# Attention and int8 feed-forward block: Q and K projected transposed, V in one pass, softmax sums through DRAM, loops unrolled

## The chip, the core and the metric

The kernel runs on one core of one Trainium2 chip, written in Bass: each engine has its own instruction stream, ordered only by semaphores. PE is TensorE, DVE is VectorE, ACT is ScalarE, POOL is GpSimd, SP is SyncE, which issues most DMAs. The metric is device time in microseconds (us), lower is better.

## The reference

X has shape (4, 1024, 512): batch, rows, columns. With 16 query heads, 8 key and value heads, head size 64 (all fp32):

```python
q = (X @ Wq)...; k = (X @ Wk)...; v = (X @ Wv)...      # per head
q = q * cos + rotate_half(q) * sin                     # k the same
att = einsum('bhqd,bhkd->bhqk', q, k) * 256.0 ** -0.5  # k, v repeated twice
att = 50 * tanh(att / 50); causal mask; softmax
y = einsum('bhqk,bhkd->bhqd', att, v) @ Wo
x = layernorm(X + y)
q8, scale = per-row absmax quantisation of x to int8
x = layernorm(x + float16(q8 @ weight.T * scale * w_scale + bias))
```

## The kernel before, in words

**Number format.** Matmul operands in float32r lose low bits, so each fp32 operand is held as a rounded high part and a low part (the value less its high part), and a product takes three matmuls (two in the scores, where both parts of Q or K lie stacked in the 128 partitions of one operand).

**Stages of a batch.** (1) The first pair: for key head j=0, `project(b, j, t)` (L441 to L463) multiplies a 128-row tile of x with the columns of two query heads, a key head and a value head together: 12 matmuls with 256 moving columns. `rope` (L800) rotates on VectorE, keeps v in two parts; `turn_qk` (L465) turns Q and K on TensorE, ScalarE's `round_qk` (L659) and VectorE's `split_qk` (L829) read the turned tiles. (2) Attention: per key head j there are nine score tiles k (`score`, L480), each 128 keys by up to 1024 (head, query) columns in two PSUM banks. A tile goes through tanh (`cap`, L669) and exp (`exponent`, L680) on ScalarE, the causal mask on GpSimd (`mask`, L1021), rounding on VectorE (`round_probs`, L840), the low part on VectorE (even k, L850) or on GpSimd (odd k, L1035), and into `weigh` (L498), which adds the value product and the softmax sum up in PSUM. Steps of the projection of head j+1 are strung between the tiles of head j; the last head has none. When a quarter of the queries is complete, ScalarE keeps the sums (L686), TensorE turns them (`turn_sums`, L522), and VectorE divides into y (L855). (3) The rows: for each of eight row tiles t, TensorE turns y (L530), ScalarE and VectorE make its two parts (L695, L870), `project_out` (L545) multiplies with Wo (24 matmuls with 512 columns), VectorE adds x and takes statistics (`residual1`, L878), GpSimd makes the inverse standard deviation (`inverse_std`, L1042), then follow normalising, quantising (L901), the int8 product in bf16 (L570), the second residual on GpSimd (L1051), second normalising and the store from ScalarE's queue (L713). Order on VectorE in row t: shift of row t-1, low part of y of row t+1, quantise row t-1, second statistics of row t-3, rescale row t-2, shift, residual of row t (L974 to L987). On GpSimd: both inverse deviations and then the second residual (L1082 to L1088).

**What sets the order.** Every engine's order is written out by hand; each waits in order. Score tiles alternate between two PSUM halves (a tile waits until the tanh of the tile two back has read), probabilities go round three buffers. The loops over batches are hardware loops (`Fori`) for the first three batches, with the last one written behind them; at the end of a batch the first pair of the next is projected between the last steps of the rows (`next_rows_steps`, L363).

## Time and profile before

| | |
|---|---|
| median of 3 runs | 1562.99 us (1562.66 to 1565.54) |
| span of the profiled execution | 1559.7 us (the profile gives no time of its own beside its span) |
| PE busy | 1415.9 us, 91% |
| DVE busy | 1272.7 us, 82% |
| ACT busy | 986.5 us, 63% |
| POOL busy | 546.2 us, 35% |
| mean granted TensorE clock | 0.974 |
| DMA | 55.98 MB, mean 36 GB/s |

Busy shares are over the whole span, of one profiled execution. Matmuls are pipelined, so the duration of one is longer than its share of a stream of them; the chain of waits gives the latter.

### The profile page before, as it was taken

The numbers are of one execution on the slowest core, as the hardware profiler recorded it, in microseconds if no ns is written. First come the engines' busy times: TensorE is split into PE (matmuls) and PEld (weight loads), VectorE is DVE, ScalarE is ACT, GpSimd is POOL, SyncE is SP. The second block draws the span as 40 slices with busy tenths as digits, with TensorE's granted clock in tenths as the row PEclk, the third lists the DMA queues.
The fourth block names the chain that finished last, engine by engine and source line by source line (L and its number), as shares of the span: only waits on it lengthen the run. The fifth ranks groups of instructions, "written<-read, shape, count | busy, mean of one in ns | idle before, by whom it ended". The sixth has DMA issues, their size and how long they took to land.

```text
span 1559.7 us, 26316 instructions
## 1 busy us (share of the span) xinstructions
PE 1415.9 (91%) x8576; PEld 1141.8 (73%) x8576; DVE 1272.7 (82%) x3228; ACT 986.5 (63%) x1374; POOL 546.2 (35%) x529
## 2 busy tenths in 40 slices
PE   3699999989789999998969999998997999999894
PEld 3588878757678887866768788885776888888572
DVE  7888888867878888885788888887678888888575
ACT  5577777763367777784337777777335777777632
POOL 2433333333323333332433333333242333333434
PEclk9899999999989999999989999999999999999997
DMA  7300000311100000032110000002210000000211
GB/s 236 129 1 1 1 1 1 109 63 52 49 9 1 1 1 1 1 108 75 44 53 1 1 1 1 1 1 108 81 53 36 1 1 1 1 1 1 108 55 41
DMA packets 25337, 55.98 MB, mean 36 GB/s; under 512 B 3824, under 2 KB 12528, under 8 KB 23920
## 3 DMA queue, kind: packets, MB, share of 16 engines
q1 hardware_dynamic: 20592, 45.88, 8.6%
q10 hardware_dynamic: 4608, 8.39, 1.4%
q8 instruction: 72, 1.18, 0.3%
q14 instruction: 65, 0.53, 0.1%
HBM read 41.68 MB, written 12.58 MB: 35 GB/s over the span
## 4 chain that ended last, share of the span: by engine, by line
PE 58%; issue 12%; DVE 12%; ACT 11%; POOL 6%; DMA 0%; ACTq 0%; POOLq 0%; DVEq 0%; SPq 0%
PE ps L516 19%; PE ps L460 16%; PE ps L492 13%; PE ps L559 4%; ACT qkT L664 4%; ACT probs L677 4%; PE ps L526 3%; ACT sums L693 2%; POOL rstd L1048 1%; POOL f L1056 1%; DVE qkT L834 1%; DVE stats L938 1%; PE ps L476 1%; PE ps L477 1%; POOL prob_lo L1039 1%
## 5 line engine op out<-in xcount | busy, mean ns | idle before, releaser
L1039 POOL TENSOR_TENSOR prob_lo<-probs,prob_hi 128x1024 fp32r<-128x1024 f32 x128 | 310.8, 2428 | 559.6 <-DVE prob_hi L848 559.6
L460 PE MATMUL ps<-w_split,xT 128*128 128x256 f32 x3072 | 420.4, 288 | 30.2 <-DVE xT L788 22.3
L460 PEld LDWEIGHTS ps<-w_split,xT 128*128 128x128 f32 x3072 | 404.9, 195 | 48.1 <-issue 22.3
L516 PE MATMUL ps<-prob_hi,v 128*65 128x512 f32 (+3 forms) x1280 | 425.1, 381 | 13.8 <-POOL prob_lo L1039 12.0
L677 ACT ACTIVATE probs<-ps 128x1024 f32<-128x1024 f32 x288 | 295.4, 1026 | 160.9 <-PE ps L492 152.9
L492 PE MATMUL ps<-qkT 128*128 128x512 f32 (+1 forms) x1280 | 322.0, 378 | 14.9 <-DVE qkT L834 14.9
L683 ACT ACTIVATE probs<-probs 128x1024 f32<-128x1024 f32 x288 | 305.5, 1061 | 8.8
L492 PEld LDWEIGHTS ps<-qkT 128*128 128x128 f32 x1280 | 229.3, 193 | 73.8 <-DVE qkT L834 16.1
L664 ACT ACTIVATE qkT<-ps 64x256 fp32r<-64x256 f32 x512 | 193.5, 378 | 106.9 <-PE ps L477 101.6
L848 DVE CAST prob_hi<-probs 128x1024 fp32r<-128x1024 f32 x288 | 203.2, 706 | 54.1 <-POOL probs L1031 26.1
L834 DVE TENSOR_TENSOR qkT<-ps,qkT 64x256 fp32r<-64x256 f32 x512 | 215.1, 420 | 35.0 <-ACT qkT L664 26.8
L516 PEld LDWEIGHTS ps<-prob_hi,v 128*65 128x65 f32 (+1 forms) x1280 | 172.9, 136 | 95.8 <-POOL prob_lo L1039 15.4
L516 PE MATMUL ps<-prob_lo,v 128*65 128x512 f32 (+1 forms) x640 | 238.0, 372 | 0.0
L852 DVE TENSOR_TENSOR prob_lo<-probs,prob_hi 128x1024 fp32r<-128x1024 f32 x160 | 198.1, 1238 | 5.5
L559 PE MATMUL ps<-wo,y_his 128*128 128x512 f32 x512 | 167.1, 406 | 3.9 <-DVE y_lows L872 3.9
L1031 POOL TENSOR_SCALAR_AFFINE_SELECT probs<-probs 128x256 f32<-128x256 f32 (+1 forms) x192 | 95.4, 505 | 182.5 <-ACT probs L683 182.4
L693 ACT ACTIVATE sums<-ps 65x512 f32<-65x512 f32 x128 | 75.4, 589 | 84.4 <-PE ps L516 83.7
L559 PEld LDWEIGHTS ps<-wo,y_his 128*128 128x128 f32 x512 | 93.9, 188 | 25.8 <-issue 5.7
L516 PEld LDWEIGHTS ps<-prob_lo,v 128*65 128x65 f32 x640 | 87.7, 137 | 25.2 <-issue 0.8
L825 DVE TENSOR_TENSOR rot<-rot,rot_sin 128x96 f32<-128x96 f32 x256 | 94.7, 370 | 8.8
L559 PE MATMUL ps<-wo,y_lows 128*128 128x512 f32 x256 | 100.5, 393 | 0.0
L710 ACT ACTIVATE probs<-probs,shift,rstd 128x512 f32<-128x512 f32 x32 | 26.1, 815 | 113.6 <-DVE shift L898 113.6
(60 smaller groups left out, 1415.3 us busy)
## 6 DMA issues: line engine op xcount, KB each, us to landing
wo<-wo_split SPq DMA_DIRECT2D x8, 2048.0 KB, 7.5
x_raw<-X_T SPq DMA_DIRECT2D x16, 512.0 KB, 5.9
x_in<-X SPq DMA_DIRECT2D x32, 256.0 KB, 3.1
result<-probs ACTq DMA_DIRECT2D x32, 256.0 KB, 2.0
wo_split<-y SPq DMA_DIRECT2D x2, 2048.0 KB, 7.3
y<-L_attn_Wq SPq DMA_DIRECT2D x4, 512.0 KB, 6.6
y<-L_attn_Wo SPq DMA_DIRECT2D x1, 2048.0 KB, 10.4
y<-L_attn_Wk SPq DMA_DIRECT2D x4, 256.0 KB, 6.8
```

What stands on the lines that cost most here:

```text
L460: mm = nc.tensor.matmul(ps[:, proj_bank(j, t), 0:QKV], xT[:, a, k, rows], w_split[:, w, k, j, :], start=(k == 0 and a == w == 0), stop=(k ...
L492: mm = nc.tensor.matmul(scores[:, g % 2, col:col + REP * n].rearrange("p (h q) -> p h q", h=REP), qkT[:, j % 2, 2 + part, keys], qkT[:, j ...
L516: mm = nc.tensor.matmul(sums_ps[:, :, GQ - n:GQ], v[:, j % 2, kt, w0:w1], p[:, g % ring, col:col + REP * n].rearrange("p (h q) -> p h q", ...
L559: mm = nc.tensor.matmul(bank, (y_lo(t) if a else y_hi(t))[:, k, :], wo[:, w, k, :], start=(n == 0), stop=(n == 3 * KO - 1))
L664: cp = nc.scalar.activation(qkT[dst:dst + HD, j % 2, n, rows].rearrange("p (i c) -> p i c", i=2), turned_qk(j, t)[src:src + HD, :, part, : ...
L677: nc.scalar.activation(probs[:, g % PRING, :], scores[:, g % 2, :], ACT.Tanh, scale=SCORE_SCALE / SOFTCAP).then_inc(capped, 1)
L683: nc.scalar.activation(probs[:, g % PRING, :], probs[:, g % PRING, :], ACT.Exp, scale=SOFTCAP).then_inc(exped, 1)
L693: nc.scalar.activation(sums[0:LOW, :], ps[0:LOW, PV_BANK + c % 2, :], ACT.Copy).then_inc(sums_kept, 1)
L834: sub = nc.vector.tensor_tensor(qkT[dst:dst + HD, j % 2, n, rows].rearrange("p (i c) -> p i c", i=2), turned_qk(j, t)[src:src + HD, :, par ...
L848: nc.vector.tensor_copy(prob_hi[:, g % 2, :], probs[:, g % PRING, :]).then_inc(rounded, 1)
L852: nc.vector.tensor_tensor(prob_lo[:, g % PRING, :], probs[:, g % PRING, :], prob_hi[:, g % 2, :].bitcast(F32), ALU.subtract).then_inc(low_ ...
L1039: nc.gpsimd.tensor_tensor(prob_lo[:, g % PRING, :], probs[:, g % PRING, :], prob_hi[:, g % 2, :].bitcast(F32), ALU.subtract).then_inc(low_ ...
```

## The change

- **Projection of Q and K.** The weights are now the stationary operand and x the moving one, so that Q and K come out turned. Work goes in 8 x 2 = 16 units m (four per batch), each for two key heads and four query heads, in three chunks x: K of all rows (x=0), Q of the first and of the second half of the rows (x=1, 2), 24 matmuls with 512 columns each. Weight columns are sorted so that the two halves of the rotation come in different partitions (K) or banks (Q). They are split once, stored to a DRAM scratch and loaded per unit into `w_ring`.
- **Rotation.** VectorE reads PSUM times cosine and sine (turned tables, made at the start on TensorE) into `work`; GpSimd adds or subtracts (`rotate`), ScalarE rounds (`round_rope`), VectorE takes the low part (`rope_low`), all over 1024 columns.
- **Layout by DMA.** `put` on SP copies both parts from `work` to the places that the scores read: eight DMAs of 32 partitions for each chunk and part, 48 per unit. Two units' Q and K are held.
- **V.** All heads in one pass, twelve matmuls with 512 columns per row tile. For the next batch it runs between attention and rows.
- **Softmax sums.** The undivided y, already turned, and the sums go to DRAM (three DMAs a group). After attention the sums come back as one 128x128 tile, one reciprocal is taken, stored and read back broadcast by two DMAs per row tile on ScalarE's queue; y is read per row tile and GpSimd multiplies (`scale_y`) before ScalarE and VectorE make the two parts. TensorE's turns of Q, K, sums and y go.
- **Chunks in time.** The chunks of unit m are projected in unit m-1's tiles (steps 0 to 2, 5 to 7, 9 to 11 of 18), except units 0, 5, 9 and 13: unit 0 before all, the others in the last rows of the batch before. The split of the next x moves to the last four steps of the third unit.
- All loops are unrolled.

The core of the diff:

```diff
@@ tensor
-                for k in range(KC):
-                    for a, w in ((0, 0), (0, 1), (1, 0)):
-                        mm = nc.tensor.matmul(ps[:, proj_bank(j, t), 0:QKV], xT[:, a, k, rows],
-                                              w_split[:, w, k, j, :], ...
-                mm.then_inc(projected, 1)
+            def project(m, x, lo, hi):
...
+                products = [(n, k, w, a) for n in range(2) for k in range(KC) for w, a in ((0, 0), (0, 1), (1, 0))]
+                for n, k, w, a in products[lo:hi]:
+                    half, slot = (n, 0) if x == 0 else (x - 1, 1 + n)
+                    mm = nc.tensor.matmul(ps[:, bank + n, :], w_ring[:, slot, w, k, :],
+                                          xT[:, a, k, half * HT:(half + 1) * HT], ...
+            for b in range(B):
+                more = b + 1 < B
+                for u in range(UB):
+                    m = chunk_unit(b, u)
+                    for s in range(2 * NS):
+                        g = u * 2 * NS + s
+                        score(b, g)
+                        if m is not None:
+                            for x, at in enumerate((0, 5, 9)):
+                                if at <= s < at + 3:
+                                    project(m, x, 8 * (s - at), 8 * (s - at) + 8)
+                        if g >= 2:
+                            weigh(b, g - 2)
+                if more:
+                    project_v(b + 1, 0)
+                weigh(b, NB - 2)
+                if more:
+                    project_v(b + 1, 1)
+                weigh(b, NB - 1)
+                if more:
+                    for t in (2, 3, 4):
+                        project_v(b + 1, t)
+                for t in range(NT):
+                    if t == 1 and more:
+                        for n in (5, 6, 7):
+                            project_v(b + 1, n)
@@ vector
+            def rope_read(m, x):
+                dve.wait_ge(projected, chunks_upto(m, x))
+                if m == 0:
+                    dve.wait_ge(tables_kept, 2)
+                    dve.wait_ge(w_stored[UB - 1], 16)
...
+                    nc.vector.tensor_tensor(turned, halves, cos_q, ALU.mult)
+                    nc.vector.tensor_tensor(crossed, swapped, sin_q, ALU.mult).then_inc(proj_read, 1)
+            def rope_low(m, x):
+                dve.wait_ge(rope_hi, chunks_upto(m, x))
+                nc.vector.tensor_tensor(work_r[:, x, 0, :], work[:, x, 0, :], work_r[:, x, 1, :].bitcast(F32),
+                                        ALU.subtract).then_inc(rope_lo, 1)
+            def invert(b):
+                dve.wait_ge(div_loaded, 16 * (b + 1))
+                nc.vector.reciprocal(div[:, :], div[:, :]).then_inc(div_done, 1)
@@ gpsimd
+            def rotate(m, x):
+                pool.wait_ge(proj_read, chunks_upto(m, x))
...
+            def scale_y(b, t):
+                pool.wait_ge(y_loaded[t % YRING], ring_upto(b, t, YRING))
+                pool.wait_ge(rb_loaded, 32 * rows_upto(b, t))
+                nc.gpsimd.tensor_tensor(y_raw[:, t % YRING, :, :], y_raw[:, t % YRING, :, :], rb[:, :, :],
+                                        ALU.mult).then_inc(y_scaled, 1)
+                for t in range(1, NT):
+                    inverse_std(b, t - 1, 0, mv1, veps1, rstd1, z_done)
+                    if t + 1 < NT:
+                        scale_y(b, t + 1)
+                    if t >= 3:
+                        inverse_std(b, t - 3, 1, mv2, veps2, rstd2, normed)
+                    if t >= 2:
+                        residual2(b, t - 2)
@@ scalar
+            def load_rb(b, t):
...
+                    act.wait_ge(y_scaled, rows_upto(b, t - 1))
+                for h in range(REP):
+                    act.dma_start(rb[h * HD:(h + 1) * HD, :, :].rearrange("p k n -> p (k n)"),
+                                  r_scratch[t, h].rearrange("k n -> (k n)").partition_broadcast(HD)
+                                  ).then_inc(rb_loaded, 16)
                 for t in range(1, NT):
+                    if t + 2 < NT:
+                        load_rb(b, t + 2)
                     if t + 1 < NT:
-                        split_y(b, t + 1)
+                        round_y(b, t + 1)
@@ sync
+            def put(m, x, low):
+                sp.wait_ge(rope_lo if low else rope_hi, chunks_upto(m, x))
...
+                    else:
+                        cols = slice((x - 1) * HT, x * HT)
+                        for r in range(REP):
+                            h = REP * i + r
+                            for half in range(2):
+                                src = work_r[32 * h:32 * (h + 1), x, 1 - low, half * HT:(half + 1) * HT].bitcast(F32)
+                                r0 = 64 * low + 32 * half
+                                sp.dma_start(buf[r0:r0 + 32, i, r, cols].bitcast(F32), src
+                                             ).then_inc(q_put[m % 2][x - 1][i], 16)
```

## Rows read from the trace of the kernel before

**Rows 1.** The page, part 4: chain that ended last, shares by engine.
```profile
PE 58%; issue 12%; DVE 12%; ACT 11%; POOL 6%; DMA 0%; ACTq 0%; POOLq 0%; DVEq 0%; SPq 0%
```

**Rows 2.** Windows: stretch, busy us (instructions) of each engine, clock, DMA share, GB/s.
```profile
60.00:300.00 240.00, 236.07 (x1519) 195.44 (x1520) 213.36 (x580) 179.44 (x254) 83.11 (x67) 1.00 0.01 2
1441.50:1472.00 30.50, 26.27 (x134) 17.29 (x133) 18.40 (x29) 25.16 (x28) 14.82 (x11) 1.00 0.23 78
```

**Rows 3.** Timeline of TensorE: start, duration, first and last score tiles of stretches.
```profile
54.82 2.08 PE L492 MATMUL ps<-qkT 128*128 128x512 f32 x6 [3.39 <-DVE qkT L834]
...
334.11 1.09 PE L492 MATMUL ps<-qkT 128*128 128x512 f32 x4
...
432.09 2.08 PE L492 MATMUL ps<-qkT 128*128 128x512 f32 x6 [3.83 <-DVE qkT L834]
...
1441.50 1.09 PE L492 MATMUL ps<-qkT 128*128 128x512 f32 x4
...
1469.21 1.09 PE L492 MATMUL ps<-qkT 128*128 128x512 f32 x4
```

**Rows 4.** Chain in order of time, in attention: start, share in the chain, instructions.
```profile
188.17 1.43 PE ps L460 x12
189.60 1.38 PE ps L516 x6
190.98 0.92 PE ps L492 x4
```

**Rows 5.** The page, part 5: groups in attention; busy us, mean ns, idle before.
```profile
L1039 POOL TENSOR_TENSOR prob_lo<-probs,prob_hi 128x1024 fp32r<-128x1024 f32 x128 | 310.8, 2428 | 559.6 <-DVE prob_hi L848 559.6
...
L677 ACT ACTIVATE probs<-ps 128x1024 f32<-128x1024 f32 x288 | 295.4, 1026 | 160.9 <-PE ps L492 152.9
...
L683 ACT ACTIVATE probs<-probs 128x1024 f32<-128x1024 f32 x288 | 305.5, 1061 | 8.8
...
L848 DVE CAST prob_hi<-probs 128x1024 fp32r<-128x1024 f32 x288 | 203.2, 706 | 54.1 <-POOL probs L1031 26.1
...
L852 DVE TENSOR_TENSOR prob_lo<-probs,prob_hi 128x1024 fp32r<-128x1024 f32 x160 | 198.1, 1238 | 5.5
...
L1031 POOL TENSOR_SCALAR_AFFINE_SELECT probs<-probs 128x256 f32<-128x256 f32 (+1 forms) x192 | 95.4, 505 | 182.5 <-ACT probs L683 182.4
L693 ACT ACTIVATE sums<-ps 65x512 f32<-65x512 f32 x128 | 75.4, 589 | 84.4 <-PE ps L516 83.7
```

**Rows 6.** Timeline of VectorE and GpSimd: a cast beside a subtract, an add.
```profile
1465.33 2.38 POOL L1039 TENSOR_TENSOR prob_lo<-probs,prob_hi 128x1024 fp32r<-128x1024 f32 x1 [0.81 <-DVE prob_hi L848]
1466.44 1.82 DVE L848 CAST prob_hi<-probs 128x1024 fp32r<-128x1024 f32 x1 [1.19 <-ACT probs L683]
...
L825 DVE TENSOR_TENSOR rot<-rot,rot_sin x256: 257/259/7720, 28.2 to 1438.7; 128x96 f32<-128x96 f32 x128
```

**Rows 7.** Timeline of VectorE in the rows of batch 0: statistics, then amax.
```profile
350.12 0.18 DVE L892 BATCH_NORM_AGGREGATE mv<-stats 128x2 f32<-128x6 f32 x1
...
372.03 0.18 DVE L892 BATCH_NORM_AGGREGATE mv<-stats 128x2 f32<-128x6 f32 x1 [0.15 <-DVE stats L889]
...
374.87 0.68 DVE L908 TENSOR_REDUCE amax<-z 128x1 f32<-128x512 f32 x1
...
405.70 0.18 DVE L892 BATCH_NORM_AGGREGATE mv<-stats 128x2 f32<-128x6 f32 x1 [0.15 <-DVE stats L889]
```

**Rows 8.** DMA issues: count, KB each, median us to landing; one issue on SP.
```profile
wo<-wo_split SPq DMA_DIRECT2D x8, 2048.0 KB, 7.5
...
x_in<-X SPq DMA_DIRECT2D x32, 256.0 KB, 3.1
result<-probs ACTq DMA_DIRECT2D x32, 256.0 KB, 2.0
...
346.63 0.34 SPq L402 DMA_DIRECT2D sums<-L_ffn_w_scale  x1
```

**Rows 9.** Windows: the start of batch 1's scores; the clock is third from the end.
```profile
432.00:434.00 2.00, 1.91 (x6) 1.59 (x6) 0.25 (x2) 0.81 (x1) 0.00 (x0) 0.50 0.05 12
```

More of the change, by code:

```diff
@@ new lines, in bias_upto, with unit_scored, wait_put, ring_upto @@
+        def bias_upto(b):
+            return 16 * (min(b, B - 2) + 1)
+        def unit_scored(m):
+            return scores_upto(m // UB, (m % UB + 1) * 2 * NS - 1)
+        def wait_put(eng, m, x):
+            for i in range(2):
+                eng.wait_ge(k_put[m % 2][i] if x == 0 else q_put[m % 2][x - 1][i], puts_upto(m))
+        def ring_upto(b, t, ring):
+            return 16 * (b * len(range(t % ring, NT, ring)) + t // ring + 1)
+        def between(m):
+            return m == 0 or (m % UB == 1 and m > 1)
@@ L363, in next_rows_steps, with chunk_unit, group_in @@
-        def next_rows_steps(work, tail, b, after):
-            for u in range(NT + 2):
-                if b is not None:
-                    work(b, u)
-                for step, t in tail.get(u, []):
-                    step(after, t)
+        def chunk_unit(b, u):
+            m = UB * b + u + 1
+            return m if m < U and not between(m) else None
+        def group_in(b, g):
+            if g < 3:
+                return None
+            j, s = divmod(g - 3, NS)
+            return (j, LAST_TILE.index(s)) if s in LAST_TILE else None
@@ L520, in weigh @@
+                            start=(first and not low and p is prob_hi), stop=True, skip_group_check=True)
                 mm.then_inc(pv_done, 1)
-            def turn_sums(b, j, c):
-                pe.wait_ge(sums_kept, groups_upto(b, j, c))
-                for n in range(2 * REP):
-                    mm = nc.tensor.transpose(group_ps(c)[:, n, :], sums[0:LOW, n * P:(n + 1) * P],
-                                             ident[0:LOW, 0:LOW])
-                mm.then_inc(sums_turned, 1)
@@ L719, in keep_q @@
                 nc.scalar.activation(q16T[:, :, :].rearrange("p k n -> p (k n)"), q16_ps, ACT.Copy).then_inc(qT_ready, 1)
[L721 to L729 removed]
+            split_x(0, 0)
+            act.wait_ge(wv_raw_in, 16)
@@ new lines, in _ @@
+            split_x(0, 1)
+            split_x(0, 2)
+            split_v(0, 0)
+            split_v(0, 1)
+            split_x(0, 3)
+            split_v(0, 2)
+            split_v(0, 3)
+            dve.wait_ge(w_hi_done, 1)
+            for x in range(2):
+                nc.vector.tensor_tensor(stages[0][:, 0, 1, :, x * HD:(x + 1) * HD].rearrange("p k (h d) -> p k h d", h=2),
+                                        raw_k_half(0, x),
+                                        stages[0][:, 0, 0, :, x * HD:(x + 1) * HD].rearrange("p k (h d) -> p k h d", h=2)
+                                        .bitcast(F32), ALU.subtract)
@@ L996, in _ @@
[L996 to L1006 removed]
+                m = UB * b + UB + 1
+                stats2(b, NT - 3)
```

1173 lines of the change are left out of this document (700 added, 473 removed).

## The prediction, made before the change was run

> **What bounds the kernel now.** I read the chain of waits of the page first, then the windows by stage, then single instructions in order of time. TensorE owns 58% of the chain that ended last [rows 1], but that share mixes stages. In the long attention stretch it is busy 236 of 240 us, so it bounds; in the last head pair of the last batch, which has no projection beside it, it is busy 26.3 of 30.5 us and ScalarE 25.2 [rows 2]. The scores start at 54.8 us, the last score tile of batch 0 ends at 335.2, and the next batch starts at 432.1 [rows 3]: 280 us of attention and 97 us between (row phase and the next first pair). The last score tile of all ends at 1470.3, 89.4 us before the end. Three stages of 97, one of 89.4 and the start of 54.8 leave 1559.7 - 435.2 = 1124.5 us for four attentions. The reader is to see that the two kinds of stage have different limits: a cheaper projection pays in the first, anything serial costs in the second.
>
> **The change, part by part.**
>
> 1. *Projection.* Twelve matmuls of 256 moving columns take 1.43 us; score and value tiles with 512 columns run at 0.23 us each (six in 1.39) [rows 4]. Now a pair of heads costs 8 x 1.43 = 11.4 us there, 9 x 2.32 = 20.9 in score and value tiles and the rest in transposes of rotated tiles and sums, which go: (280.4 - 34) / 7 = 35.2 us a pair, where 34 is the last pair, 27.7 [rows 3] and an estimated 6 for the split of the next x in it. The new unit of two pairs has 18 tiles at 0.93 + 1.39 = 2.32 us, and 72 projection matmuls at 0.23 = 16.6: a floor of 58.3 us against 70.4. Units without a projection (unit 0 of batches 1 to 3, unit 3 of batch 3: four of 16) have a floor of 41.8 on TensorE and of 18 x (1.03 + 1.06) + 8 x 0.59 = 42.3 on ScalarE [rows 5].
>
> 2. *The port.* This is where I don't take TensorE's floor. A VectorE cast that should take 0.69 us began at 1466.44, while a GpSimd subtract ran to 1467.71, and took 1.82; an add with both inputs in SBUF, 0.26 us at its median, took 7.72 once [rows 6]. So VectorE's casts and its operations with two SBUF inputs take turns with GpSimd's. Per unit this turn-taking work is now 8 x 2.43 (low parts on GpSimd), 12 x 0.505 (masks), 18 x 0.69 and 10 x 1.23 on VectorE [rows 5]: 19.4 + 6.1 + 12.4 + 12.3 = 50.2 us, against 70.4 of TensorE. The change adds per unit three rotations on GpSimd (1024 columns each, 2.43) and three low parts on VectorE (1.23): +11.0, so 61.2 us, more than TensorE's 58.3. The check on this is the last pair of the kernel: half of 50.2 is 25.1, and its nine tiles took 1469.21 - 1441.50 = 27.7 us [rows 3], 1.10 times that, some of it waits of the turned sums which go. I take 65 us for a unit with a projection (bounds 58.3, the TensorE floor, and 75, the present one plus the delay of rotations queued ahead of masks) and 53 without (bounds 42.3 and 58). VectorE's rotary reads (PSUM in, 1.2 us per 1024 columns) and the value split have no turn to take; VectorE's own total falls, and I cost them at nothing as long as a unit stays above 55 us.
> Twelve units: 12 x (65 - 70.4) = -65. Three without projection: 3 x (53 - 70.4) = -52. The last: 53 against 35.1 + 27.7, -10. The split of the next x moves from the pair that has no projection into the middle of a unit, with the first new projection right behind it; I take +8 us in three batches, +24 (bounds 0, since the same work was there before, and 36). Attention: -103.
>
> 3. *Transition to the rows.* Now the first row statistics (350.3) come 15 us after the last score tile (335.2) [rows 3, 7]. New order after the last value tile (about 9 us after the last score): keep sums 0.6, three stores (0.34 issue each, 2.0 landing, the page's store), load of the divisors 3.1, reciprocal 0.5 (bounds 0.2 and 1), store back 2.0 plus what the 2 MB of y and x loads issued ahead of it take (2 MB lands in 7.5 us; I take 2), the broadcast load 3.1 after two issues [rows 8], then GpSimd scaling 2.43, ScalarE rounding 1.03 and VectorE 1.22: y of tile 0 is ready at about 30 us. project_out of tile 0 (24 x 0.23) runs from there, cold, since TensorE idles from 17; tile 1 is scaled meanwhile, and the first statistics come at 38. +23 us (bounds 12, where the DMAs land faster than their nearest rows, and 35). Five value projections of the next batch are hidden in this wait (5 x 2.8), costing nothing; the other three (8.3 us) stand before project_out of tile 1 and, through the order on VectorE, before row 1.
>
> 4. *Row period.* Row 3's statistics end at 372.2 and row 7's at 405.9: 8.4 us a row, and between the statistics of one row and VectorE's amax at 374.87 [rows 7] lie GpSimd's rstd and the shift. Behind that rstd GpSimd now scales y of tile t+1 (2.43), ScalarE must pass two broadcast issues (2 x 0.34) before it rounds it (1.03), and only then VectorE splits it and goes on to amax: 2.43 + 0.7 + 1.03 + 0.1 = +4.3 a row, 12.7 us. TensorE then idles over 4 us a row; at 432 us its clock stands at 0.50 (1.2 GHz) after 3.8 us of idling [rows 9], which would put the second half of project_out some 0.5 us late. 13.2 a row. Counted out over rows 1 to 7, with the shorter first two and the last, the statistics of row 7 come 88 us after those of row 0 against 55.6 now (405.9 - 350.3): +32 (bounds +20 if scaling slips into idle time in half the rows, +45 if every row's project_out runs cold). For the last batch +27.
>
> 5. *Tail to the next attention.* Projection, rotary and puts of unit 1 stand between row 7 and the first tanh, but unit 0's Q and K lie ready since the batch before. GpSimd rotates between its last statistics, VectorE reads 3.65 + 2 x 2.43 us. I count 21 us against 28 now: -7 (bounds -15, +10). Puts are issued by SP: eight DMAs at 0.34 each; 48 puts and 24 sums DMAs are 72 x 0.34 = 24.5 us of issue per unit, under 65. If the unit fell to that, SP would be the next to be late, ahead of it the puts in the last three tiles.
>
> 6. *Start.* Values of batch 0, table transposes and splits of all weights come before Q and K; the first rotary read waits for the fourth weight store, since that stage shares its space. GpSimd's three low parts (1536 columns, 3.6 us each) end near 49, the store near 56, then read, rotate, round, low part and four puts in order: first score at 77 against 54.8, +22 (bounds +5, +30). Unrolled loops: nothing, bounds -5 and +5, no row of loop ends stands out.
>
> **Sum.** Start +22, three transitions of +23 + 32 - 7 = +48, the last of +23 + 27 = +50, less 2 as nothing of the next batch stands in it: +48. 22 + 144 + 48 - 103 = +111. The profiled span is 1559.7 and the runs lie 3.0 to 5.8 us above it with the median at +3.3; I add the change to that median: 1563 + 111 = **1674 us**.
>
> **Transfers.** 4 MB of puts, 1.5 MB of weights and about 0.5 MB of sums a unit need 92 GB/s in 65 us; the 2 MB transfer reached 280 GB/s [rows 8]. Small pieces from SBUF to SBUF have no row. By the Trainium skill, DMA: Bandwidth & Descriptors, section Bandwidth, transfers should be batched to 1 MiB or more, and under 64 KB they are dominated by descriptors; an estimate by the fit in that page's section Anatomy of one DMA (2.0 us and bytes by 436 GB/s) is 2.15 us for 64 KB, some 100 us a unit if they ran singly. No run here shows whether they do.
>
> **Rivals.**
> - *The port costs little.* Turns overlap better than I think and the unit runs at TensorE's floor: 12 x (58.3 - 70.4) = -145, light units at 43: -82 and -20, split +24: -223 in place of -103, total 1554, **faster**. It decides when a projecting unit takes less than 59 us. For it: TensorE has had 98% in attention. Against: the last pair took 27.7 us with 25.2 of ScalarE and 21 of TensorE needed. 0.10.
> - *Rows don't lengthen*, because scaled tiles run ahead: -4.3 x 6 x 4 = -103: 1571. Against: the GpSimd order puts scaling behind rstd of the row before. 0.12.
> - *Attention gains nothing*: rotations sit ahead of masks, units stay at 71 and 57: 12 x 6 + 4 x 4 = +88: 1762. 0.15.
> - *Transfers bound a unit*: each put holds the queue for the 2.0 us of the shortest landing, 96 us a unit, 12 x 31 = +372: 2046. Against: the rate above. 0.05.
> - *The projection isn't 0.23 a matmul* (loads from the weight ring, late): at 0.28, 12 x 3.6 + 4 x 1.4 (values) = +49: 1723, inside my own range. 0.03.
> My forecast keeps 0.55.
>
> **Numbers.** About 3 us, 0.2%, is what a measurement of this kernel can tell from no change. Low: the two gaining rivals are 0.22, and half of the row rival's spread reaches 1585 and above with other terms at their slower side. High: 1745 holds most of attention gaining nothing; the transfer rival is left out. Range 1585 to 1745; my forecast alone 1620 to 1720. Faster by over 0.2%: most of the first rival, 0.08. Within: 0.03. Slower: 0.89.
>
> **What would show it right or wrong.** In the profile of the changed kernel: first score near 77 us; score tiles 18 apart in 65 us with a projection and 53 without; casts (0.69 alone) and low parts on VectorE stretched more often; statistics of rows 13 us apart with y's low part waiting for ScalarE's rounding; TensorE busy near half in the rows and its clock down there; projection matmuls at 0.23. I am wrong if a projecting unit is under 60 us, if rows stay near 9 us apart, or if scores wait for puts.

## The result, and the profile after

The changed kernel takes 1801.42 us in the median of 4 runs, the kernel before 1562.83 us (4 runs): ratio 1.152, 95% interval 1.150 to 1.154. That is 239 us slower, where 111 were forecast. (One of the four runs of the changed kernel, at 2294 us and a clock of 0.58, was disturbed; the ratio leaves it out, and the other three are 1800.20, 1800.20 and 1802.64 us.) The profiled execution has a span of 1800.9 us.

The page of the changed kernel: busy times, the clock over 40 slices, the transfers, and the chain by engine, which answers to [rows 1]:

```profile
PE 1369.2 (76%) x5760; PEld 978.6 (54%) x5776; DVE 988.3 (55%) x1114; ACT 856.1 (48%) x952; POOL 809.5 (45%) x653
...
PEclk9799998998788999897878999989878899999686
...
q1 hardware_dynamic: 106320, 185.94, 36.0%
...
PE 34%; POOL 23%; issue 13%; DVE 12%; ACT 10%; DMA 3%; SPq 3%; ACTq 1%; POOLq 0%; DVEq 0%
```

No engine is near its limit any more: TensorE falls from 91% to 76% and VectorE from 82% to 55%. In the chain that ended last TensorE's share falls from 58% to 34%, and GpSimd's rises from 6% to 23%. TensorE, VectorE and ScalarE are busy for less time than before and only GpSimd for more (546 us before, 810 now); what got worse is the order in which they wait for one another. The timeline of TensorE gives the stages, as [rows 3] did: the first score tile of all; the starts of the second, third and fourth unit of batch 0; the last score tiles of batch 0; batch 1's first; and the last of all. (386.47 is the last three of four matmuls; what counts there is their end, 387.95.)

```profile
81.90 2.04 PE L642 MATMUL ps<-qk 128*128 128x512 f32 x6 [25.73 <-DMA qk<-work_r]
...
160.86 1.10 PE L642 MATMUL ps<-qk 128*128 128x512 f32 x6
...
235.88 1.10 PE L642 MATMUL ps<-qk 128*128 128x512 f32 x6
...
314.75 1.08 PE L642 MATMUL ps<-qk 128*128 128x512 f32 x6
...
386.47 1.48 PE L642 MATMUL ps<-qk 128*128 128x512 f32 x3
...
538.10 1.78 PE L642 MATMUL ps<-qk 128*128 128x512 f32 x9
...
1656.57 1.09 PE L642 MATMUL ps<-qk 128*128 128x512 f32 x4
```

| stage | before | forecast | after |
|---|---|---|---|
| start to first score | 54.8 | 77 | 81.9 |
| four attentions together | 1124.5 | 1021 | 1125.6 |
| between last score and next first, each of three | 97 | 145 | 150 |
| last score to the end | 89.4 | 137 | 143.2 |

The last column adds to the span: 81.9 + 1125.6 + 3 x 150.1 + 143.2 = 1801. The other stages are 5 to 6 us over the forecast each time they occur, 26 us together; attention is where a gain of 103 us was forecast and none came. A unit with a projection takes 73 to 79 us (160.86 - 81.90 = 79.0, then 75.0 and 78.9), 75.4 in the mean of the twelve (the last unit of a batch taken to the end of its last score tile), and not 65. The first unit of batches 1 to 3, which has no projection, takes 57.7 (538.10 to 595.78 in batch 1) and not 53. The waits of the changed kernel, in total us, times and longest, say what is late:

```profile
ACT y_hi L859 <- issue: 218.5, 27, 20.1
...
DVE y_lo L1034 <- ACT y_hi L859: 170.5, 32, 15.4
...
ACT work_r L809 <- POOL work L1207: 141.5, 32, 5.9
...
ACT work_r L809 <- POOL work L1202: 74.3, 16, 18.9
```

L809 is `round_rope`, L1202, L1205 and L1207 are `rotate`, L859 is `round_y`. ScalarE stands 141.5 + 74.3 = 215.8 us before its 48 roundings. How one of these waits comes about is in the timeline of ScalarE, VectorE and GpSimd in the third unit of batch 0 (some instructions left out):

```profile
272.62 1.06 ACT L825 ACTIVATE probs<-probs 128x1024 f32<-128x1024 f32 x1
273.71 1.81 POOL L1225 TENSOR_SCALAR_AFFINE_SELECT probs<-probs 128x256 f32<-128x256 f32 x3
...
275.50 2.25 POOL L1205 TENSOR_TENSOR work<-work 128x512 f32<-128x512 f32 x1
276.52 1.78 DVE L1016 CAST prob_hi<-probs 128x1024 fp32r<-128x1024 f32 x1
277.71 1.74 POOL L1207 TENSOR_TENSOR work<-work 128x512 f32<-128x512 f32 x1
278.33 2.20 DVE L1020 TENSOR_TENSOR prob_lo<-probs,prob_hi 128x1024 fp32r<-128x1024 f32 x1
279.49 1.06 ACT L809 ACTIVATE work_r<-work 128x1024 fp32r<-128x1024 f32 x1 [5.81 <-POOL work L1207]
280.45 1.01 ACT L820 ACTIVATE probs<-ps 128x1024 f32<-128x1024 f32 x1
```

GpSimd can rotate only behind the mask of the tile before, and the mask only behind that tile's exponential (ended 273.68). ScalarE's next instruction behind the same exponential is the rounding. So by the written order ScalarE waits for one mask and two rotations, 5.81 us, while the next tile's tanh (L820) stands behind the rounding; its scores are ready about 276.3 and it begins at 280.45. Three such places a unit are visible in the distances between score tiles: in the second unit of batch 0 they are 4.2 4.1 4.1 2.3 3.7 4.2 4.1 **5.6** 2.3 4.9 4.1 4.1 **5.8** 2.6 2.4 4.7 **8.1** 3.9 us; a tile needs 4.1 with a piece of projection beside it and 2.3 without.

### The profile page after: what moved, and what is told of

Read it like the earlier page. It is cut to its first block, busy times and chain, and to the rows that moved or that the text cites. A ratio compares the mean times of both kernels' runs of the same rounds, so it can differ in the third digit from the quotient of the medians.

```text
span 1800.9 us, 17417 instructions
## 1 busy us (share of the span) xinstructions
PE 1369.2 (76%) x5760; PEld 978.6 (54%) x5776; DVE 988.3 (55%) x1114; ACT 856.1 (48%) x952; POOL 809.5 (45%) x653
## 4 chain that ended last, share of the span: by engine, by line
PE 34%; POOL 23%; issue 13%; DVE 12%; ACT 10%; DMA 3%; SPq 3%; ACTq 1%; POOLq 0%; DVEq 0%
PE ps L668 11%; POOL prob_lo L1232 9%; PE ps L690 6%; PE ps L642 6%; PE ps L613 5%; PE ps L587 4%; DVE prob_hi L1016 4%; ACT probs L825 4%; ACT probs L820 3%; POOL probs L1225 3%; POOL y_raw L1238 3%; POOL work L1205 2%; SPq L429 2%; POOL work L1207 2%; PE ps L710 2%
## 5 line engine op out<-in xcount | busy, mean ns | idle before, releaser
L1016 DVE CAST prob_hi<-probs 128x1024 fp32r<-128x1024 f32 x288 | 314.6, 1092 | 375.5 <-POOL probs L1225 300.8
L642 PE MATMUL ps<-qk 128*128 128x512 f32 (+1 forms) x1280 | 331.6, 387 | 43.6 <-DMA qk<-work_r 28.5
L820 ACT ACTIVATE probs<-ps 128x1024 f32<-128x1024 f32 x288 | 293.5, 1019 | 128.8 <-PE ps L642 127.5
L642 PEld LDWEIGHTS ps<-qk 128*128 128x128 f32 x1280 | 237.4, 199 | 107.7 <-issue 45.9
L587 PE MATMUL ps<-xT,w_ring 128*128 128x512 f32 x1152 | 286.5, 394 | 4.5 <-DVE xT L968 3.0
L690 PE MATMUL ps<-wo,y_hi 128*128 128x512 f32 x512 | 197.4, 470 | 70.6 <-issue 70.6
L587 PEld LDWEIGHTS ps<-xT,w_ring 128*128 128x128 f32 x1152 | 215.5, 189 | 50.8 <-DVE xT L968 3.6
L690 PEld LDWEIGHTS ps<-wo,y_hi 128*128 128x128 f32 x512 | 115.5, 229 | 103.5 <-issue 77.8
L809 ACT ACTIVATE work_r<-work 128x1024 fp32r<-128x1024 f32 x48 | 50.9, 1061 | 215.8 <-POOL work L1207 141.5
L859 ACT ACTIVATE y_hi<-y_raw 128x1024 fp32r<-128x1024 f32 x32 | 33.8, 1057 | 248.6 <-issue 218.5
L1238 POOL TENSOR_TENSOR y_raw<-y_raw,rb 128x1024 f32<-128x1024 f32 x32 | 75.3, 2353 | 118.2 <-DMA rb<-r_scratch 118.2
L710 PE MATMUL ps<-ffn_wT,q16T 128*128 128x512 bf16 x112 | 45.8, 546 | 99.5 <-ACT q16T L879 99.3
```

The lines of the kernel that those rows point to most:

```text
L587: mm = nc.tensor.matmul(ps[:, bank + n, :], w_ring[:, slot, w, k, :], xT[:, a, k, half * HT:(half + 1) * HT], start=(k == w == a == 0), st ...
L642: mm = nc.tensor.matmul(scores[:, g % 2, col:col + REP * w].rearrange("p (h q) -> p h q", h=REP), qk[:, n % 2, i, 2 + part, keys], qk[:, n ...
L690: mm = nc.tensor.matmul(bank, (y_lo[:, t % YRING, k, :] if a else y_hi[:, t % 2, k, :]), wo[:, w, k, :], start=(n == 0), stop=(n == 3 * KO ...
L820: nc.scalar.activation(probs[:, g % PRING, :], scores[:, g % 2, :], ACT.Tanh, scale=SCORE_SCALE / SOFTCAP).then_inc(capped, 1)
L1016: nc.vector.tensor_copy(prob_hi[:, g % 2, :], probs[:, g % PRING, :]).then_inc(rounded, 1)
L1238: nc.gpsimd.tensor_tensor(y_raw[:, t % YRING, :, :], y_raw[:, t % YRING, :, :], rb[:, :, :], ALU.mult).then_inc(y_scaled, 1)
```

## The experiments

The theories were: **A**, as forecast: VectorE and GpSimd take turns, as at one shared port, and this sets the units; **B**, ScalarE stands in order behind a rotation not yet done; **C**, SyncE's queue and the landing of what it issues are late; and for the rows, that the scaling stands in each row's chain. "Attention" below is the sum of the four stretches from first to last score tile, "outside" is the rest of the span; the changed kernel has 1125.6 and 675.3. A "step" is the distance from the start of one score tile to that of the next; a unit has 18.

### e1: the rounding one tile later

```diff
-                        if m is not None and s in (5, 10, 14):
-                            round_rope(m, (5, 10, 14).index(s))
+                        if m is not None and s in (6, 11, 15):
+                            round_rope(m, (6, 11, 15).index(s))
...
-                            if s in (5, 6):
-                                put(m, 0, s - 5)
+                            if s in (6, 7):
+                                put(m, 0, s - 6)
```

The low part on VectorE and the other puts move by one tile in the same way.

> Edit: in the changed kernel the ScalarE rounding of a turned chunk, the VectorE low part behind it and the puts all come one tile later (rounding at tiles 6, 11, 15 for 5, 10, 14). No work is added or removed. Theory A (the port shared by VectorE and GpSimd holds the units at 71 to 79 us): nothing moves, 1801 within 10 us. Theory B (ScalarE stands in order before a chunk that GpSimd, busy with a mask or a low part, has not rotated yet: 215.8 us of idle ScalarE before the rounding in the changed kernel): most of these waits go, 60 to 180 us off, 1620 to 1740. Theory C (SyncE and the landing of the puts are late): the last puts of a unit are a tile later still, the next unit's first score waits for them, 12 units x 2 to 5 us, 1825 to 1860.

Measured: 1739.66 us (1738.24 to 1741.08), 62 us less. Attention 1052.7 (-73), outside 683.8 (+8.5). The waits:

```profile
ACT work_r L809 <- POOL work L1207: 52.8, 17, 5.9
ACT work_r L809 <- POOL work L1202: 44.7, 16, 18.9
```

Not one instruction was taken away and 62 us went: B, at the low end of its gain, and A alone cannot be. ScalarE's waits before the roundings are 97.5 us in place of 215.8. A unit in which nothing else disturbs (the second one of each batch) now takes 65.2, 65.0, 65.0 and 65.1 us, the 65 of the forecast. C's forecast of 1825 to 1860 fails, and no first score of a unit waits for a put that it did not wait for before; but the later puts are not free. Eight of them now stand in SyncE's queue right in front of the loads of the next x (L773 splits it), and in all ScalarE waits longer for it, first in the changed kernel and then in e1:

```profile
ACT xT L773 <- DMA x_raw<-X_T: 16.1, 5, 4.2
...
ACT xT L773 <- DMA x_raw<-X_T: 37.9, 5, 11.8
```

And at the end of a batch the first row statistics come 47.3 us behind the last score tile and no longer 43.5 (batch 0). In the last batch, which has no next puts, this distance is not longer (39.0 against 39.7). So C is right about the queue, if not about who pays: this is what e11 to e13 work on.

### e2: no low part on GpSimd

```diff
-    POOL_LOW = [s % 2 == 1 for s in range(NS)]
+    POOL_LOW = [False for s in range(NS)]
```

> Edit: all 18 low parts of the probabilities of a unit on VectorE (nine of them were GpSimd's at 2.36 us beside VectorE's 1.22). Theory A (turns at the port, so that the sum counts): 9 x (2.36 - 1.22) = 10 us off a unit, 16 units, 160 off at most, about 1650 to 1720, and the unit without projection shows it too (24.6 us per nine tiles falls to about 20). Theory B: the masks and rotations find GpSimd free sooner, so the waits before the rounding shrink from 3.5 to 5.9 us to 1 to 2: about 2 to 3 us x 3 x 12 units, 70 to 110 off, 1690 to 1730, but the unit without projection gains nothing. If neither holds and VectorE's order is what counts: slower, 9 x 1.22 us more work on it per unit, up to 1950.

GpSimd had eight of the 18 low parts of a unit (128 in 16 units), not the nine of the expectation. Measured: 1713.87 us (1711.57 to 1716.17), 87.6 less; attention 1030.0. Projecting units take 66.9 us (second ones), and the first units of batches 1 to 3, without projection, 54.1 against 57.7. The last nine tiles of such a unit fall from 24.8 to 22.5 us, against a TensorE floor of 20.9. The total lies in the ranges of both theories. The unit without projection gains 3.6 us, which B alone does not give, but its nine tiles gain only half of what A expected (2.3 us of 4.6). By itself this run does not decide between them.

### e3: the rotation left out

```diff
-                    nc.gpsimd.tensor_tensor(work[:, x, 0, 0:HT], work[:, x, 0, 0:HT], work[:, x, 1, 0:HT],
+                    nc.gpsimd.tensor_tensor(work[:, x, 0, 0:8], work[:, x, 0, 0:8], work[:, x, 1, 0:8],
```

and the two others in the same way.

> Edit: the GpSimd additions that finish the rotation of a chunk are cut to 8 columns each, so most of the rotation of Q and K is left out (the instructions and semaphores stay); this prices the rotations. Theory A: 3 x (2.2 + 1.7) = 11.7 us of the port off a unit, 13 units of attention, about 150 off, 1650. Theory B: the wait of ScalarE shrinks to what the mask ahead leaves, about 2 us each of 3.5 to 5.9: 2 to 4 us x 39 chunks, 80 to 150 off, 1650 to 1720. Theory C: nothing in attention, 1790 to 1801.

This kernel leaves out the rotation of all but 8 columns in each addition, so Q and K are not what they should be, and the run only prices the rotations. Measured: 1711.52 us (1710.57 to 1712.46), 90 less, in B's range and far from the 150 of A; attention 1039.7. ScalarE's waits before the rounding fall from 215.8 to 107.7 us and no further: the mask is still in front. So about half the wait is the rotation itself and half what stands before it. The run takes the rotations off the port as well, and does not tell the two effects apart. A later place (e1) gives 62 of the 90 without leaving anything out.

### e4: rows scaled a tile further ahead

```diff
                 scale_y(b, 1)
+                scale_y(b, 2)
...
-                    if t + 1 < NT:
-                        scale_y(b, t + 1)
+                    if t + 2 < NT:
+                        scale_y(b, t + 2)
```

On ScalarE, `load_rb(b, t + 3)` now comes right behind `norm1(b, t - 1)`.

> Edit: in the row phase GpSimd scales the sums of tile t+2 instead of t+1 and ScalarE issues the load of the reciprocals of t+3 right behind the normalisation of t-1. Row theory (the chain load of the reciprocals, GpSimd scaling, rounding, subtraction, projection is a row's period of 13.8 us in place of 8.45): the rows come 8.5 to 10 us apart, 4 to 5 us x 6 rows x 4 batches = 95 to 130 us off, 1670 to 1705. Rival (the engines' own work in a row, or the landing of 4 us of the reciprocals, is the period): less than 1.5 us a row, 1765 to 1801. The attention phases stay as they are in all cases.

Measured: 1722.63 us (1721.85 to 1723.41), 79 less, and all of it outside attention (1126.0 and 595.7). The ends of the row statistics of batch 0 in this kernel:

```profile
428.25 0.18 DVE L1051 BATCH_NORM_AGGREGATE mv<-stats 128x2 f32<-128x6 f32 x1
441.85 0.18 DVE L1051 BATCH_NORM_AGGREGATE mv<-stats 128x2 f32<-128x6 f32 x1
448.54 0.18 DVE L1051 BATCH_NORM_AGGREGATE mv<-stats 128x2 f32<-128x6 f32 x1
463.68 0.18 DVE L1051 BATCH_NORM_AGGREGATE mv<-stats 128x2 f32<-128x6 f32 x1
473.17 0.18 DVE L1051 BATCH_NORM_AGGREGATE mv<-stats 128x2 f32<-128x6 f32 x1
...
500.44 0.18 DVE L1051 BATCH_NORM_AGGREGATE mv<-stats 128x2 f32<-128x6 f32 x1
```

From row 4 on a row takes (500.44 - 473.17) / 3 = 9.1 us instead of 13.7, so the row theory holds. Row 3 still takes 15.1, and the chain of waits says why (start, share of the chain):

```profile
436.82 12.26 DMA rb<-r_scratch
...
450.02 2.34 POOL y_raw L1239
```

The reciprocals of that row need 12.26 us instead of 4.0. Beside them run the next weights (1.5 MB) and the broadcast bias. That is the likely reason why 79 us came and not 95 or more; e11 tests it.

### e9, e5, e7: together

e9 is e1 and e2 together. e5 is e2 with the rotation moved to VectorE, right behind its reads of PSUM, and without e1. e7 is e9 and e4.

> Edit: the two edits of e1_rounding_later and e2_low_on_vector together (rounding one tile later; no low part on GpSimd). Theory B (the in-order wait of ScalarE was what both removed, in part the same microseconds): a projecting unit at 62 to 65 us (e1 65.2, e2 66.9), together 90 to 115 us off the changed kernel's 1801, not 62 + 88 = 150: 1690 to 1710. Theory A (turns at the port as well): the two add up, units at 59 to 60 us, 1640 to 1665.

> Edit: from the changed kernel, the low parts of e2 and also the rotations on VectorE, right behind its two multiplications; GpSimd keeps only the masks. ScalarE then never waits for GpSimd before a rounding. Theory B: the stalls at steps 8, 13 and 17 of a unit go, and those at the start of a batch (7.1 and 8.8 us, where the third chunk is rotated between two masks) too: unit with projection 61 to 64 us, first unit of a batch 48 to 52, 1620 to 1670. Rival (VectorE is then in the way: 34 us of casts and subtractions, 11 of rotation reads and low parts, 7 of rotations in a unit of 58, and rope work in front of a cast holds a tile by 3.7 us): units 66 to 70 us, 1710 to 1760.

> Edit: e9 and the row phase of e4 (scaling a tile further ahead). The row phase and the attention phase do not overlap, so e4's 79 us should come off in full on top of e9: if e9 is x, this is x - 79 within 8.

Measured: e9 1693.63 us (1691.39 to 1695.88), e5 1685.76 (1684.98 to 1686.53), e7 1621.82 (1621.77 to 1621.88). e9 is in B's range and far from A's. Its attention is 996.5, 129 less, but outside it has 693.2, 18 more: part of the gain in attention is given back behind it. The three stages between batches, in which 16 puts stand before the last sums, are 156.2 to 157.2 us for 150.1, and the end of the last batch, which has no such puts, is not longer (141.9 for 143.2). The unit is at 62.1 us, in B's range too. e5 fell between both ranges. Its units are nearly where B had them, 63.9 with a projection and 51.7 to 52.1 without; the first two steps of a batch take 6.7 us together and the third 7.6, in place of 7.0 and 8.8. The rope work on VectorE now holds up two tiles a unit (4.8 us at the fifth step, 3.9 at the fourteenth). Its attention is 998.9, but outside it has 685.9, 11 more than the changed kernel, and that the expectation had not counted. e7 took 71.8 off e9, at the edge of the 8 us given: attention and rows add up.

### e11, e10: SyncE's order

e11 is e7 and three changes of the order of SyncE's queue; it adds and removes nothing:

```diff
+                load_y(b, 0)
+                sp.wait_ge(div_done, b + 1)
+                sp.dma_start(r_scratch.rearrange("t h j n -> (t h j) n"), div[:, :]).then_inc(div_stored, 16)
-                for t in range(YRING):
+                for t in range(1, YRING):
                     load_y(b, t)
                 for t in range(XRING):
                     load_x(b, t)
-                sp.wait_ge(div_done, b + 1)
-                sp.dma_start(r_scratch.rearrange("t h j n -> (t h j) n"), div[:, :]).then_inc(div_stored, 16)
```

The four loads of the next x go ahead of `load_wq` and `put(m, 1, 1)`, and `load_wk`, `load_wq` move from row 1 to row 4.

> Edit: e7, and only the order of SyncE's queue changed: the four loads of the next batch's x ahead of the second put of chunk 1 and of the load of weights; the store of the reciprocals ahead of the loads of the second and third tile of sums and of x; the weights of the next chunks loaded at tile 4 of the rows instead of 1. Theory C in its weak form (SyncE's 0.6 us a put makes the loads behind it late): x lands 5 to 6 us earlier (3 batches), the first row starts 2 to 4 us earlier (4 batches), and the reciprocals of row 3, which took 12 us to land beside the weights, take 4 (3 batches, 5 us each): 30 to 50 us off e7's 1622, 1572 to 1592. Rival (these loads are bound by something else, such as ScalarE's own queue): within 8 us of 1622.

> Edit: e11, and the rotations on VectorE as in e5, and the third chunk of a batch's next unit rounded three tiles later (tile 5 of a batch for 2). Expected beside e11: 8 us off from the rotations (e5 against e9), 3 x 3 us from the later rounding (steps of 7.2 and 8.8 us at the start of a batch): 10 to 20 us below e11, 1555 to 1580. That is where it would beat the kernel before (1563) or just miss it. Rival: VectorE, now in order with 53 us of work in a unit of 58, takes the gain back and it equals e11.

Measured: e11 1583.61 us (1582.66 to 1584.55), 38.2 less than e7, as C in its weak form said; the rival is out. In the third unit of a batch the step that waited for x falls from 14.2 to 3.9 us, row 3 comes 10.0 us after row 2 instead of 15.7, the store of the reciprocals lands in 1.5 us instead of 6.3. The three reorderings were made together; attention gives 24 us of the gain and the rest 15. e10 took 1597.90 us (1597.36 to 1598.44), 14 more than e11, a miss of the forecast: its attention is 990.1 against 975.9. VectorE's cast is shorter without rotations on GpSimd (0.74 us in the mean against 0.99 in attention of batch 0), but 4 us of rotations a unit in front of the casts cost more than that (the fifth and the fourteenth step of a unit are 4.8 and 3.6 us instead of 3.7 and 2.3). The later rounding of the third chunk gave nothing: the first units of batches 1 to 3 take 54.8, 54.9 and 55.7 us against 54.9, 55.5 and 55.6. The rival in the expectation said "equal"; it is worse than that.

### e12, e13: the end of a batch

In e11 SyncE's queue at the end of batch 0 shows what the last sums stand behind:

```profile
339.87 11.12 SPq L429 DMA_DIRECT2D qk<-work_r  x16
...
351.03 1.29 SPq L441 DMA_DIRECT2D y_scratch<-sums  x2
...
352.36 0.64 SPq L444 DMA_DIRECT2D d_scratch<-sums  x1
353.05 0.40 SPq L527 DMA_DIRECT2D wo<-wo_scratch  x1
353.49 1.42 SPq L441 DMA_DIRECT2D y_scratch<-sums  x2
354.95 0.62 SPq L444 DMA_DIRECT2D d_scratch<-sums  x1
360.84 0.32 SPq L532 DMA_DIRECT2D div<-d_scratch  x1
```

Sixteen puts, which nobody needs for 130 us, take 11.1 us; then a load of 2 MB gets in front of the last sums, which take 5.3 us to land. In e12 the eight puts of the high parts stay where they are; of the eight of the low parts four follow the load of the output weights on SyncE, and four go to ScalarE's queue. ScalarE also rounds the first row before it issues the second load of reciprocals:

```diff
+                if b + 1 < B:
+                    put(UB * b + UB, 2, 1, (0,))
                 put_sums(b, NKV - 1, G - 1)
...
+                if more:
+                    put_low(UB * b + UB)
                 keep_sums(b, NKV - 1, G - 1)
```

`put_low` issues the four transfers of the low parts for the second key head. e13 is e12 with `sp.wait_ge(rb_loaded, 32 * rows_upto(b, 0))` in front of the loads of the second and third tile of sums and of x.

> Edit: e11, and at the end of a batch the 2 MB load of the output weights and the sums' own transfers no longer stand behind 16 puts of the next batch's Q (11.1 us in SyncE's queue in e11, issued from 339.87 to 351): half of those puts go behind the load of the output weights, half to ScalarE's queue, which is idle there; and ScalarE rounds the first row before it issues the second load of reciprocals. Theory C in its weak form: the last sums land in about 2 us instead of 5.3, the first row starts 5 to 7 us earlier in three batches, 1 us of the rounding in each: 16 to 24 us off 1583.6, 1560 to 1568, level with the kernel before (1563). Rival (the division and the two loads of reciprocals are what the first row waits for): within 5 us of 1583.6.

> Edit: e12, and SyncE waits for the first reciprocals to land before it issues the loads of the second and third tile of sums and of x (1.5 MB) at the start of a row phase. In e12 those reciprocals landed 7.4 us after their issue, against 4.0 in the median. If the loads in front of them are the cause: 3 us off at each of four batches, 12 us less than e12's 1575.7, 1560 to 1568, level with the kernel before. Rival (the second tile of sums and x come late instead, and the first two rows wait for them): within 5 us of e12, or above it.

Measured: e12 1575.72 us (1568.89 to 1582.77, 6 runs), 7.9 less than e11 where 16 to 24 were expected; its runs spread more than those of the others. The first row statistics come at 387.0 instead of 389.7. The last sums leave at 352.64 instead of 353.49, less than 1 us earlier, since eight puts and the load of 2 MB still stand in front of them; they still take 4.9 us to land, and the first two transfers of reciprocals take 6.8 and 7.9 us where the median of the changed kernel is 4.0. So the edit moved less of the queue than the expectation had counted on. e13: 1569.21 us (1565.09 to 1574.6, 12 runs), 6.5 less than e12 where 12 were expected (the ranges of the runs overlap, the means are 7 us apart). The two transfers take 3.4 and 3.9 us, and GpSimd begins to scale the first tile at 367.86 instead of 372.66. Against the kernel before the ratio is 1.0035, interval 1.0021 to 1.0050: still slower, by some 5 us.

### e14: the port by itself

e12 with the low parts of e2 back on GpSimd.

> Edit: e12 with the nine odd low parts of a unit back on GpSimd (the edit of e2 undone, everything else kept: rounding late, rows scaled ahead, SyncE's order). This prices the port alone, with the in-order waits gone. Theory A as forecast (turns at the port add up to 61.2 us a unit with the low parts there and 51 without): units with projection 65 against 62, light ones 3.5 us longer: 12 x 3 + 4 x 3.5 = 50 us above e12, 1615 to 1635. Rival (the port costs nothing once nobody stands in order, all 12 units stay at 62): 1570 to 1585.

Measured: 1611.97 us (1609.14 to 1614.8), 36 above e12. Attention is 1025.9 against 976.5, +49 where A said 50. Of it 33 us are in the twelve units with a projection and 16 in the four without (36 and 14 expected). Outside, 587.2 against 598.3 gives 11 back, the cause of which stays open, and this puts the total just under A's range. The starts of the second and the third unit of batch 1, in e14 and then in e12, from TensorE's timeline:

```profile
537.97 1.09 PE L647 MATMUL ps<-qk 128*128 128x512 f32 x6
...
603.00 1.09 PE L647 MATMUL ps<-qk 128*128 128x512 f32 x6
```

```profile
527.31 1.09 PE L647 MATMUL ps<-qk 128*128 128x512 f32 x6
...
589.41 1.09 PE L647 MATMUL ps<-qk 128*128 128x512 f32 x6
```

65.0 us against 62.1. The rival (1570 to 1585) is out. The port is a real price, some 3 us a unit for eight low parts on GpSimd. The forecast had that price in its 65 us; it is not what made the difference to the measured time.

| kernel | median | attention | outside |
|---|---|---|---|
| before | 1562.8 | 1124.5 | 435.2 |
| changed | 1801.4 | 1125.6 | 675.3 |
| e1 | 1739.7 | 1052.7 | 683.8 |
| e2 | 1713.9 | 1030.0 | 684.4 |
| e9 (e1, e2) | 1693.6 | 996.5 | 693.2 |
| e7 (e9, e4) | 1621.8 | 999.9 | 620.1 |
| e11 | 1583.6 | 975.9 | 605.0 |
| e13 | 1569.2 | 975.9 | 587.5 |

Attention and outside are of the profiled executions and add up to their spans, not to the medians. For e13 the profiled execution is the fastest of the twelve (1565.09 us).

## Why the prediction failed, by its steps

- **Sign and direction** were right: slower, 0.89. The time was not: 1801 lies above the range's 1745.
- **Step 1, projection**: held. The tile with a piece of projection takes 4.1 us, 2.32 + 1.84 for eight matmuls at 0.23, in every kernel here.
- **Step 2, the price of a unit, is the step that failed: it has no term for the time that ScalarE waits in order.** The rotations were summed up as load on a port, and ScalarE entered with its busy time alone (42.3 us a unit). Nothing was counted for its wait, at a written place, for a mask and a rotation on GpSimd, with the next tanh behind it. Measured, a unit with a projection takes 75.4 us in the mean and not 65; moving the rounding by one tile (e1) takes 73 us out of attention and puts the undisturbed unit at 65.0 to 65.2. The full diff has it: `rotate` at steps 4, 9, 13 and `round_rope` at 5, 10, 14, with one exponential in front of both.
- **The 65 itself is in part luck.** The port's sum of 61.2 us was checked against the last head pair of the kernel before, "nine tiles in 27.7 us". But 1441.50 is the last tile of the pair before. The last pair begins here:

```profile
1446.22 1.10 PE L492 MATMUL ps<-qkT 128*128 128x512 f32 x6
```

  Its eight steps to 1469.21 take 23.0 us, or 25.9 for nine tiles, which is 1.03 times the 25.1 of the sum and not 1.10. With the factor of this check the unit would have been 63 us. By the same slip the unit before the change was put at 70.4 us; it took 72.2. This moves the forecast of attention by 5 us only, since its units were set as times and not as differences.
- **The rival "attention gains nothing"** (0.15, units at 71 and 57, 1762) was right in size: units at 73 to 79 and 57.7. Its price was 17 us short in attention (1125.6 against its 1021 + 88 = 1109), and the other 22 to 1801 are the stages outside. Its mechanism, "rotations sit ahead of masks", as also in the upper bound of 75, is not what happened. In the timeline of GpSimd in the changed kernel no mask begins over 0.3 us behind its exponential with a rotation just before it (with a low part just before it, 51 do, 62.9 us in all). The rotation stands behind the mask, and the queue that is held up is ScalarE's. So a chance higher than 0.15 would have been right for the time and wrong for the reason.
- **The 104 us between forecast and result in attention**: the twelve units with a projection are 100 over theirs (the 24 for the split of x counted in), the three first units 14 (57.7 for 53; their first two steps take 7.0 us together and the third 8.8, where the third chunk is rotated between two masks), the last unit 5 under, and the 5 us of the slip above go off. Of the 100, 73 went with e1. The split of the next x costs some 7 us a batch in the changed kernel, where 8 were counted, but 15 in e1 (third units 75 to 76 us for 65, and 9 us for 4 in the first step behind): its loads stand behind puts of 0.63 us each. In e11, where they stand in front, it is 5 to 7.
- **Step 3, into the rows**: 43.5 us from the last score tile to the first statistics, 38 forecast. The store of the reciprocals lands in 6.2 us, where 2 + 2 had been counted for it.
- **Step 4, row period**: 13.7 us in the middle rows against 13.2 forecast, rows 0 to 7 in 90.9 (522.16 - 431.29) against 88. The mechanism was the forecast one, and e4 confirms it. The two statistics are:

```profile
431.29 0.18 DVE L1050 BATCH_NORM_AGGREGATE mv<-stats 128x2 f32<-128x6 f32 x1
...
522.16 0.18 DVE L1050 BATCH_NORM_AGGREGATE mv<-stats 128x2 f32<-128x6 f32 x1
```

- **Step 5**: from row 7 to the next first score 15.8 us against 21. SyncE's issue was undersized: 0.34 us was the price of a load, a put costs 0.63 and a store of sums 0.64. 72 of them are 45 us a unit and not 24.5. It did not bound a unit. It made the loads of x and the last sums late, more so with the later puts of e1, and e11 to e13 got this back.
- **Step 6**: 81.9 against 77.
- **Transfers bound a unit** (0.05) did not happen. Its time to landing was right, but a put holds the queue for 0.63 us and not for 2.0. The page of the changed kernel gives 2.0 us to landing for 64 KB.

```profile
qk<-work_r SPq DMA_DIRECT2D x256, 128.0 KB, 2.3
qk<-work_r SPq DMA_DIRECT2D x512, 64.0 KB, 2.0
```

By the Trainium skill, DMA: Bandwidth & Descriptors, section Anatomy of one DMA, the estimate was 2.15 us for 64 KB, and the trace agrees (2.0), though that fit is stated for transfers issued by GpSimd and these are SyncE's. Eight puts are issued in 5.00 us, each landing in about 2.0, so they overlap and do not add up: with 48 puts a unit, what is felt is the time that they take in SyncE's queue.

Could more be had? With the rounding later, the low parts on VectorE, the rows scaled ahead and SyncE's queue in another order, 232 of the 239 us come back (e13), which leaves it 5 to 6 us behind the kernel before. It has 149 us less attention (975.9 against 1124.5) and 152 us more outside, of which the start is 27, and the rest the way of the sums through DRAM (row 0 comes 43 us behind the last score, 15 before). The value projection, which was in attention before, stands there too. What is left is thus an exchange: cheap projection against serial work between the batches. Whether the way through DRAM can be shortened further was not tried.

## What to carry to other kernels

When a change adds a step on one engine between two steps on another, write down for each waiting instruction what it is behind and what is behind it, on its own engine, at that exact place in the order; a sum of loads, even a right one, says nothing on that. A step of the chain that nobody needs for a while belongs a tile later; look first at what it then stands in front of (here the loads of x and the last sums, in SyncE's queue). In a queue that issues transfers, the count times the issue time is the delay of whatever comes next, and the urgent one goes first.

## What the runs showed of the hardware

- **A VectorE cast waits for GpSimd to end.** The cast takes 0.69 us alone. In the changed kernel, beside a rotation:

```profile
256.20 2.40 POOL L1202 TENSOR_TENSOR work<-work 128x1024 f32<-128x1024 f32 x1
256.26 2.89 DVE L1016 CAST prob_hi<-probs 128x1024 fp32r<-128x1024 f32 x1 [2.86 <-POOL probs L1225]
```

It began 0.06 us behind the addition and ended at 259.15, 0.55 behind the addition's end at 258.60. That is close to its time alone, counted from the addition's end: it did not share, it waited. The Trainium skill, SBUF — State Buffer, section SBUF: two separate sides, calls this an exclusive lock and not a split of bandwidth; this row agrees. The mean of 288 casts rose from 0.71 us [rows 5] to 1.09.
- **Issue time depends on the transfer**: on SyncE 0.32 to 0.43 us for most loads, 0.74 for one of the turned x (4 in 2.95), 0.63 for a put of 32 partitions from SBUF to SBUF (8 in 5.00), 0.64 for a store of sums; on ScalarE 0.55 for a broadcast load (2 in 1.10).
- **Landing depends on what is in front**: 64 KB of reciprocals land in 6.2 us behind loads of y and x and in 1.5 in front of them; the broadcast of 256 KB in 4.0 in the median, in 7.9 (e12) and 12.3 (e4) beside other loads, and in 3.9 with those loads held back (e13).
- **The granted clock** of TensorE is lower where TensorE idles more: 0.974 in the mean before, 0.889 in the changed kernel, 0.941 in e13. In the attention of batch 0 it is 0.99, 0.93 and 0.98, with TensorE busy for 96%, 82% and 91% of the stretch; so the waits cost some time at the lower clock as well, which no run here prices by itself.
